# Graph attention by scans: weight and decay exponents from one PSUM bank, and gathers issued three chunks ahead

## The reference

```python
f_src, f_dst, f_v = feat @ W_src.T + b_src, feat @ W_dst.T + b_dst, feat @ W_v.T + b_v
a = f_src[src] + f_dst[dst]
e = where(a >= 0, a, 0.2 * a)
ex = exp(e - segment_max(e, dst)[dst])
sa = ex / segment_sum(ex, dst)[dst]
rst = segment_sum(f_v[src] * sa, dst)
```

## Time and profile before

| | |
|---|---|
| median of 3 runs | 4202.26 us (4187.69 to 4205.66) |
| the profiled execution, its own time | 4217.84 us |
| its span, from first to last instruction | 4216.0 us |
| PE busy | 2904.7 us (69%) |
| DVE busy | 2103.0 us (50%) |
| POOL busy | 1590.1 us (38%) |
| ACT busy | 780.2 us (19%) |
| DMA moved | 725.77 MB, 172 GB/s on average |
| attention stage, from the first to the last scan of the maximum | 2605.58 to 3888.71 us |

### The profile page before, as it was taken

One profiled execution on the slowest core, in us unless ns is written; L12 is line 12 of the kernel. 1 busy time (PEld: TensorE's weight loads), 2 busy tenths in 40 slices (PEclk: granted clock), 3 DMA queues, 4 the chain that ended last, 5 costly groups with the idle time before them and its releaser, 6 DMA issues.

```text
span 4216.0 us, 49450 instructions
## 1 busy us (share of the span) xinstructions
PE 2904.7 (69%) x14303; PEld 1742.8 (41%) x14451; DVE 2103.0 (50%) x4819; ACT 780.2 (19%) x1986; POOL 1590.1 (38%) x1665
## 2 busy tenths in 40 slices
PE   1444534444444666879677774999999999999188
PEld 1333323333333221434322222666666666666044
DVE  4555565555555322331300122777777777777420
ACT  0001101010100000100010011444444444444100
POOL 1656436666666100030000006555555556554200
PEclk6555555555555899889899956999999999999597
DMA  9940094000000899013179704778777878786142
GB/s 393 374 154 1 5 358 153 1 1 1 1 1 1 330 407 372 0 59 103 57 268 320 264 25 133 230 239 241 239 235 241 242 237 247 235 244 203 57 142 72
DMA packets 460279, 725.77 MB, mean 172 GB/s; under 512 B 64483, under 2 KB 334862, under 8 KB 460206
## 3 DMA queue, kind: packets, MB, share of 16 engines
q1 hardware_dynamic: 388154, 611.92, 41.6%
q0 software_dynamic: 65680, 109.05, 9.8%
q10 hardware_dynamic: 6372, 3.91, 0.3%
HBM read 443.75 MB, written 280.94 MB: 172 GB/s over the span
## 4 chain that ended last, share of the span: by engine, by line
PE 46%; DVE 18%; another core or an unknown queue 12%; DMA 11%; issue 7%; ACTq 2%; ACT 2%; POOL 1%; DVEq 1%; SPq 0%; POOLq 0%
DMA G<-adj_d 11%; PE PS L559 7%; DVE G L1225 6%; PE PS L738 5%; DVE G L1224 5%; PE PS L767 4%; PE PS L762 4%; PE PS L794 3%; PE PS L796 3%; PE PS L795 3%; PE PS L761 2%; PE PS L746 2%; PE PS L829 1%; PE PS L711 1%
## 5 line engine op out<-in xcount | busy, mean ns | idle before, releaser
L511 POOL DMA_INDIRECT adj_d<-D,place x782 | 748.8, 958 | 636.3 <-DVE place L1236 439.1
L498 POOL DMA_INDIRECT G<-tab_sv,src_e x784 | 748.7, 955 | 538.7 <-issue 288.4
L605 PE MATMUL PS<-wst,G 128*128 128x4 bf16 x1564 | 104.3, 171 | 637.2 <-DVE G L1225 600.2
L595 PE MATMUL PS<-ident,kst 128*128 128x128 f32 x1564 | 464.9, 453 | 86.8 <-ACT wst L1030 60.0
L595 PEld LDWEIGHTS PS<-ident,kst 128*128 128x128 f32 x1564 | 361.4, 321 | 92.8 <-ACT wst L1030 60.3
L1224 DVE SCALAR_TENSOR_TENSOR G<-PS,kst,tri 128x128 bf16<-128x128 f32 x782 | 271.0, 347 | 251.6 <-remote 146.9
L605 PEld LDWEIGHTS PS<-wst,G 128*128 128x128 bf16 x1564 | 72.3, 107 | 749.7 <-DVE G L1225 600.5
L1225 DVE TENSOR_SCALAR G<-PS,kst 128x256 bf16<-128x256 f32 x782 | 371.8, 475 | 0.0
L1440 DVE TENSOR_TENSOR_SCAN RB<-mring,RB,PS 128x512 f32<-128x512 bf16 x196 | 251.2, 1281 | 150.7 <-issue 78.9
L1029 ACT ACTIVATE kst<-G 128x2 f32 (+1 forms) x391 | 79.4, 203 | 1085.9 <-DVE place L1236 948.5
L528 POOL DMA_INDIRECT run_d<-V,head_i x25 | 24.0, 959 | 677.4 <-ACT V L1108 670.0
(11 more groups left out here) (324 smaller groups left out, 4871.9 us busy)
## 6 DMA issues: line engine op xcount, KB each, us to landing
G<-adj_d SPq DMA_DIRECT2D x350, 512.0 KB, 5.7
frac_d<-OSF SPq DMA_DIRECT2D x196, 512.0 KB
adj_d<-RB SPq DMA_DIRECT2D x7, 12800.0 KB, 54.5
run_d<-RB SPq DMA_DIRECT2D x4, 12992.0 KB
VT<-run_d SPq DMA_DIRECT2D x196, 256.0 KB
mring<-cut_d SPq DMA_DIRECT2D x196, 128.0 KB
HTx<-seg_d SPq DMA_DIRECT2D x196, 128.0 KB
OSF<-cnt_d SPq DMA_DIRECT2D x42, 512.0 KB
```

Of the source, the lines that this page charges most:

```text
L498: pool.indirect_dma_start(dest, None, table, bass.IndirectOffsetOnAxis(ap=idx, axis=0)).then_inc(done, 16)
L511: pool.indirect_dma_start(adj_d, bass.IndirectOffsetOnAxis(ap=place[:, w, k:k + 1], axis=0), pay[:, w, k, :], None).then_inc(sgr[g % 2], 16)
L595: last = nc.tensor.matmul(PS[:, r % 2, k * P:(k + 1) * P], kst[:, r, k:k + 1].to_broadcast([P, P]), ident[:, :], start=True, stop=True)
```

## The change

1. The block of the exponents (L794 to L797) used to write two banks: decay = m[e] - m[e+1] + cut in bank 4 + q by three matmuls (two fp32, one bf16), weight = score - m[e+1] in bank q by one fp32 matmul. Now it forms only one quantity, x = score - m[e] - cut, in bank q, by one fp32 and one bf16 matmul. The PE's wait for the numerator scan of chunk c - 2 goes, since it no longer writes bank 4 + q.
2. Since m[e+1] = max(m[e] + cut, score), the weight is exp(-relu(-x)) and the decay is exp(-relu(x)). ACT computes these by four activations where it had two: relu(-x) into D01, relu(x) into bank 4 + q (`gx`), then, after a wait for its own `gx`, the two exponentials in place (new semaphore `gp`). ACT now waits for the numerator scan of chunk c - 2 ahead of all four.
3. DVE's weight times value waits for `gp` in place of `gx`. PE's front still waits for `gx`, which now comes after the two relus.
4. POOL waits, before the gathers of chunk c, until PE has read chunk c - 3, not c - 4.

```diff
-        identb = sb("identb", [P, P], bf16)
+        nidentb = sb("nidentb", [P, P], bf16)
...
                 for c in range(NC):
                     h = c % R
-                    if c >= R:
-                        pool.wait_ge(ga, c - R + 1)
-                        pool.wait_ge(gv, c - R + 1)
+                    if c >= R - 1:
+                        pool.wait_ge(ga, c - R + 2)
+                        pool.wait_ge(gv, c - R + 2)
...
-                        if not (first and h < 2):
-                            pe.wait_ge(gback, GB * (c - 2) + GB)
-                        nc.tensor.matmul(PS[:, 4 + q, :], ident[:, :], RB[:, q * CE:(q + 1) * CE], start=True, stop=False)
-                        nc.tensor.matmul(PS[:, 4 + q, :], nident[:, :], RB[:, q * CE + 1:(q + 1) * CE + 1], start=False, stop=False)
-                        nc.tensor.matmul(PS[:, q, :], nident[:, :], RB[:, q * CE + 1:(q + 1) * CE + 1], start=False, stop=True, skip_group_check=True)
-                        nc.tensor.matmul(PS[:, 4 + q, :], identb[:, :], mring[:, h, :], start=False, stop=True).then_inc(dif, 1)
+                        nc.tensor.matmul(PS[:, q, :], nident[:, :], RB[:, q * CE:(q + 1) * CE], start=False, stop=False, skip_group_check=True)
+                        nc.tensor.matmul(PS[:, q, :], nidentb[:, :], mring[:, h, :], start=False, stop=True, skip_group_check=True).then_inc(dif, 1)
...
                         act.wait_ge(dif, c + 1)
-                        nc.scalar.activation(PS[:, 4 + q, :], PS[:, 4 + q, :], ACT.Exp)
                         if not (first and h < 2):
                             act.wait_ge(gback, GB * (c - 2) + GB)
-                        nc.scalar.activation(D01[:, q, CE:2 * CE], PS[:, q, :], ACT.Exp).then_inc(gx, 1)
+                        nc.scalar.activation(D01[:, q, CE:2 * CE], PS[:, q, :], ACT.Relu, scale=-1.0)
+                        nc.scalar.activation(PS[:, 4 + q, :], PS[:, q, :], ACT.Relu).then_inc(gx, 1)
+                        act.wait_ge(gx, c + 1)
+                        nc.scalar.activation(D01[:, q, CE:2 * CE], D01[:, q, CE:2 * CE], ACT.Exp, scale=-1.0)
+                        nc.scalar.activation(PS[:, 4 + q, :], PS[:, 4 + q, :], ACT.Exp, scale=-1.0).then_inc(gp, 1)
...
                     q = h % 2
-                    dve.wait_ge(gx, c + 1)
+                    dve.wait_ge(gp, c + 1)
                     dve.wait_ge(gv, c + 1)
```

More of the change, by code:

```diff
@@ L281, in build @@
         gx = sem("gx")
+        gp = sem("gp")
         gfront = sem("gfront")
@@ L1279, in _ @@
                 v.tensor_scalar(hdj[:, j, :], hd[:, :], float(-j * CW), None, ALU.add)
-            step(v.tensor_copy(identb[:, :], ident[:, :]))
+            step(v.tensor_copy(nidentb[:, :], nident[:, :]))
             dve.wait_ge(pst, 7)
```

## The result

The changed kernel takes 4370.62 us (median of 4 runs, 4365.24 to 4388.44), the kernel before beside it 4203.96 (4 runs, 4187.69 to 4226.44): a ratio of 1.040, 95% interval 1.0343 to 1.0457. It is slower by 167 us; 229 us faster was forecast.

What follows compares the result with a forecast made beforehand. PE was taken as the bound, 6.30 us of a 6.58 us turn. Steady 5.1 plus 0.28 of stalls made 5.4, saving 231 less 2 over 196 turns: 3989 us as profiled, 3973 as median; range 3905 to 4085.

Steps and rivals of the forecast that it cites:

- PE, 4.57 us: PE's turn in the attention stage falls from 6.30 to 4.57 us, as two fp32 blocks of 1.73 us go.
- DVE, 4.84 us: DVE's unchanged work in an attention turn takes 4.84 us if it never waits, about 5.3 at the upper end.
- POOL 5.0, DMA 5.0 to 5.1, steady turn 5.1: Per attention turn: four gathers 5.0 us with small delays, transfers 5.0 to 5.1, giving a steady turn of 5.1.
- Rival A: Attention-stage transfers become the bound at recorded packet time, 5.7 us a turn: 4084 us, 4050 to 4100; chance 0.15.
- ACT's chain, covered by 1.2 us: Latency from exponents block to DVE's L1412 grows by 1.12 to 2.28 us, hidden with 1.2 us of cover.
- The gathers' lead, cost 0: Gathers three chunks ahead have 11.1 us before PE's front and need 8.5: cover 2.6, cost taken as 0.
- The stalls, kept as a constant 0.28 us a turn: Stalls of unnamed cause in the attention stage, 55 us in all, stay at 0.28 us a turn.
- the chance of 0.02 for a gain lost to something unseen: Chance 0.02 that something not seen eats the gain, leaving the whole kernel within 0.5% of before.
- POOL's idle time: POOL's standing between two chunks' gathers in the attention stage, 1.22 us, was said to be only PE's lead.
- Rival D: PE's clock falls to 1.2 GHz in the attention stage: 9.42 us a turn with stalls, 4760 us; chance 0.03.
- Rival E: POOL's gathers slow as DVE fills up: 5.92 us an attention turn with stalls, 4075 us; chance 0.03.
- The bounds 3892 and 4084: Limits of the forecast: 5.0 us an attention turn without stalls, 3892; 5.98 by recorded packet times with stalls, 4084.

Runs made afterwards that it cites:

- e9: Changed kernel with two gathers a chunk in place of four (output not the reference's): 3853.85 us against 4163.43 for the kernel before, ratio 0.9252.
- e10: Changed kernel, gathers replaced by one plain SP load of 512 fixed rows a chunk: 3853.91 us against 4163.43 for the kernel before, ratio 0.9256.
- e1: Changed kernel with only its fourth part undone (gathers four chunks ahead again): 3406.51 us against 3649.2 for the kernel before, ratio 0.9326.
- e6: Kernel before with two fp32 blocks of the exponents left out (output not the reference's): 4353.89 us against 4207.31, ratio 1.0347.
- e2: Kernel before with only the fourth part of the change (gathers three chunks ahead): 3649.54 us against 3649.2, ratio 0.9992.
- e7: Changed kernel with gathers four chunks ahead again, same text as e1 in another set: 4316.96 us against 4163.43 for the kernel before, ratio 1.0377.
- e5: Changed kernel again, unaltered: 4356.36 us against 4207.31 for the kernel before, ratio 1.0367.
- e12: Changed kernel, gathers of chunk c started only after PE's front of chunk c - 2: 3535.54 us, ratio 0.9656 to the kernel before.
- e4: Changed kernel, POOL waiting before each chunk's third gather for the exponents block of three chunks before: 3426.41 us against 3649.2, ratio 0.9383.
- e8: Same kernel as e4 (wait before each chunk's third gather) in another set: 4117.83 us against 4163.43 for the kernel before, ratio 0.9892.
- e14: Changed kernel with plain SP loads for gathers, plus 784 one-word GpSimd gathers that nothing waits for: 3424.76 us, ratio 0.9373 to the kernel before.
- e18: Same kernel as e14 (plain SP loads plus 784 unused one-word gathers), run again: 3417.05 us, ratio 0.9366 to the kernel before.
- e13: As e12, and the fourth gather of a chunk also waits for the values of chunk c - 2: 3520.4 us, ratio 0.9654 to the kernel before.

## Why the prediction was wrong

Point by point, by its own steps:

- **PE, 4.57 us.** Right: 4.57 from L793 to L793 above.
- **DVE, 4.84 us.** Right: 4.83 and 4.84 in e9 and e10, where nothing else bounds.
- **POOL 5.0, DMA 5.0 to 5.1, steady turn 5.1.** Right where no release is late: e1's whole turn is 5.07. POOL hardly stood for PE there (6.4 us in 300), the DMA share was 0.99, and DVE 95% busy, as forecast. Rival A's 5.7 did not come: 308 GB/s at a share of 0.99. In the 4200 kind, where the forecast was made, this part of it never came to bear.
- **ACT's chain, covered by 1.2 us.** Right, and only just. From L976's start to L1412's it is 2999.13 - 2996.86 = 2.27 us (2.24 were reckoned between these two points), and in e1 L1412 waits for ACT 1.7 us in 300. e6 settles that the chain is not the loss.
- **The gathers' lead, cost 0.** Not refuted: e2 (0.9992) has PE's old long turn, and e7 beside e5 (1.0377 and 1.0367, in two sets) has the stalls. Where no release is late, the changed kernel did not run as it stands. Even with the old lead (e1) PE waited 67 us of the stage for gathered rows, and 152 us in e12, which starts them later; e4, with the shorter lead and one wait more, is 20 us slower than e1. So the shorter lead costs at most little there.
- **The stalls, kept as a constant 0.28 us a turn.** This is the step that failed. Its size before was right: 6.58 - 6.29 (e2's turn) = 0.29 us. But it was no constant. In the changed kernel it is 7.42 - 5.07 (e1's turn) = 2.35 us a turn. The stalls grew by 196 x (2.35 - 0.29) = 404 us, the rest of the turn shrank by 196 x (6.29 - 5.07) = 239, and the difference is the 165 us lost. The prediction said of these stalls "I cannot name their cause and keep them as a term"; with the cause unnamed there was no ground for keeping the term, and the chance of 0.02 for a gain lost to something unseen was far too small. The other terms fit e1, but the forecast was made from a trace of the 4200 kind, and there it missed by 396 us.
- **POOL's idle time "is only PE's lead".** With PE at 6.30 us a turn POOL, with 4.98 us of gathers, came back to its wait after every chunk: fours. At 4.57 us PE runs ahead of POOL, POOL finds the next chunk free already, and fours join into eights. After a late release it finds two chunks free at once (4.47 us for PE above, then eight gathers). So the shorter PE turn makes the long runs, and a late release the next long run. That GpSimd's gathers are the cause in the 4200 kind is shown by e9 and e10, and that a run is enough without the shorter PE turn by the seven runs of seven before and in e2. How the turn's shape makes the long runs, and that their length sets the size of the delay, is argued from the counts of both traces; e8 shows that shorter runs shrink the delay and do not end it.
- **Rival D, the clock.** It fell to 0.83 in the window, not below 0.73, and PE's own turn stayed at 4.57. It is a result of the stalls, but not a small one: 68 lifts ran at the half clock, and from such a lift to the next exponents' block it is 5.91 us on average in place of 3.50, 68 x 2.41 = 164 us. They come on top of the 370 us that PE stands ahead of L768, and both are in the 404. The prediction saw the half clock behind a stall and gave it no price.
- **Rival E.** Gathers took 981 ns on average after (769.4 us in 784), against 955 before: 0.1 us a turn where E asked for 0.66. Not the cause.
- **A slip in the sum.** The bounds 3892 and 4084 leave out the 2 us that the forecast takes off; nothing hangs on it.

The Trainium skill ("GPSIMD Engine Reference", Key points), by which rival E would have decided, is not borne out here as a loss. In e1, with DVE at 95%, a gather took 968 ns on average, 13 more than before.

**What stays open.** What sets the two kinds of set apart; why a run of four delays in e8 and mostly does not in the other kernels; what makes POOL pause every 26 turns; where between matmul and waiter the release is held; whether it is the issuing on GpSimd or the packets of its queue (e14 and e18 were to tell); whether the changed kernel as it stands gains in a set of the 3650 kind as e1 does (e1, with the old lead, and e4 and e12, with more waits, ran there); whether e12's or e13's order beats e8's in the 4200 kind.

## What to carry to other kernels

A stall that the profile attributes to nothing is not a constant. Before an edit shortens the bounding engine's turn, look at what the other engines were doing in each of the stalled turns; here, in the kernel before's own trace, all 9 fronts that met the fourth or a later gather of a run were already late. Price the clock with the stall: a standstill cost PE its time and then 2.4 us more. Where GpSimd issues indirect DMAs beside a tight loop of matmuls, try a wait that breaks its runs: it cost 0.6 points of the gain in one kind of set (0.938 against 0.933) and brought 4.9 in the other (0.989 against 1.038; the versions compared differ in the lead too). And a result from one set of runs can have the other sign in the next: the same kernel text gave 0.933 and 1.038.

## What the runs showed of the hardware

- In sets of the 4200 kind TensorE's releases reach ScalarE, SyncE and VectorE 3 to 7 us behind the recorded end of the matmul, several of them at once, while GpSimd issues indirect DMAs in a row (changed kernel: 65 of 66 fronts beside the fourth or a later gather). In sets of the 3650 kind runs of up to 92 gathers delay nothing (e1).
- The kernel before takes 3650 us or 4160 to 4210 us with no change in the text. Of the difference 2605.58 - 2096.70 = 509 us lie ahead of the first scan, 506 of them in the merge step, where GpSimd scatters by indirect DMAs (1300 against 794 us from its first to its last L1224).
- A hardware queue with 512 KB loads in place of the gathers reached 326 GB/s beside a DVE that was busy 99.6% of the time (e10).
- Behind a standstill of 4.58 us TensorE ran at its lower level for more than the next block: in the changed kernel L768 took 2.07 us in place of 1.02, and from its start to the next L793 it was 6.13 us in place of 3.50.
